# A decoder layer on one core: two rounds of weight rounding moved to other steps, and one pair of maxima matmuls placed ahead of an output projection

## The chip, the core and the metric

The kernel runs on one core of a Trainium2 chip. The metric is the time of one execution on the device, in microseconds; less is better. The engines of the core are TensorE (PE in the rows; PEld is its weight load), VectorE (DVE), ScalarE (ACT), GpSimd (POOL) and SyncE (SP, here the queue that issues most DMAs). Each works through its own list of instructions in order and waits on semaphores.

## What is computed

One post-norm decoder layer on 4 sequences of 512 tokens of width 512: causal self attention with rotary position (16 heads of 32, 8 key and value heads), causal cross attention over the first 512 rows of a context of width 128, and a gated feed-forward of width 1408 whose three weights go through a 4-bit (NF4) quantisation and back. A layer norm follows each of the three.

```python
x = _layernorm(x + _L0_attn_ref(x, wq, wk, wv, wo))            # self attention
x = _layernorm(x + _L0_xattn_ref(x, ctx_512, Wq, Wkv_expand, Wout))
w1, w2, w3 = (nf4_roundtrip(w) for w in (weight1, weight2, weight3))
h = _silu(x @ w1.T) * (x @ w2.T)
x = _layernorm(x + h @ w3.T)
```

## The kernel before

The attention part runs over batches b = 0 to 7 (0 to 3 are the four sequences in self attention, 4 to 7 the same in cross attention; `crossed(b)` is b >= 4) and, in each, over pairs of heads p = 0 to 7. One such step is named (b, p) here. The order of instructions on every engine is written out by hand in these two nested loops; nothing schedules them. The feed-forward follows.

In a step, PE computes the transposed scores of the pair (`scores`, L1027), in four parts 0 to 3 whose exponentials ScalarE takes (`exponential`, L1506); it weighs the values with them (`weigh`, L1054), the last two parts of a pair in the following step; and it computes the scores of the pair two steps ahead (`maxima`, L993, four parts of two matmuls) only so that VectorE can take each row's maximum (L1709 in self, L1703 in cross attention). `turn_maxima` (L1015) transposes these maxima once a step; "from transpose to transpose" below is from one of these to the next. Beside this, a step makes a piece of the next batch (`made`, `make`: q, k and v projections at L979 to L981, transposes at L1066). For self attention POOL rotates the raw q and k (L792, L795, L797) and splits them in high and low parts (L780, L782). In step (b, 1) stands the output projection of the batch before, in two halves (`project_out`), with VectorE's residual add (`add_residual`, L1732 and L1733) and the first moments of the layer norm behind each; the rows are scaled later (`scale_rows`, L1759), in step 5 for b = 5 and 6, and stored by SP (L579).

The weights of the feed-forward are rounded to the 16 levels of NF4 meanwhile, in 48 rounds u. `round_steps` lists the step of each round; step 1 of a batch after the first has two, one in the middle (`mid`) between the halves of the output projection and one at the end (`end`). One round is:

- SP: `load_rows4` (L514) loads the source rows, repeated four times, once PE has read those of the round before; `load_scales` first stores the result of the round before in four DMAs (`store_round`, L527), then loads the scales (L521).
- Four comparison passes over a tile of 128 x 1408 in bf16, at L1484 on ScalarE or L1863 on VectorE (`exceed`). `scalar_passes` says which passes are ScalarE's: pass 0 alone, or 0 and 1 in cross steps 2, 4 and 5, or 0, 1 and 3 in self steps 3 and 4. Pass 3 writes over the source rows, so it comes after the other three.
- PE: `rounding` (L1176), 16 matmuls, 12 for passes 0 to 2 and 4 for pass 3, which wait for the passes.
- VectorE: `scale_rounded` (L1877) adds, scales and so frees the PSUM bank.

The PSUM tile `att_scores_T` has two banks that are given out in turn, in the order that `ring_order` lists; a unit waits until the unit two places ahead of it has been read. PSUM `att_scores` holds the maxima's scores, one bank for each head of the pair. `SELF_ROUNDS` is the number of rounds in self attention; these have their source rows in one buffer (`att_nf_home`), the later ones in another (in `att_probs`).

The loops also load the stacked q and k of the pair three steps ahead (`load_stacks`, L493, L497, L501, six DMAs). For the first pair of a batch this stands behind the rounding's DMAs of its step, otherwise ahead of them.

## Time and profile before

| what | before |
|---|---|
| median of 3 runs | 1099.31 us (1093.14 to 1099.64) |
| the profiled execution | 1097.65 us |
| its span in the profile | 1095.9 us, 17718 instructions |
| PE busy | 1031.4 us (94%) |
| VectorE busy | 760.2 us (69%) |
| ScalarE busy | 486.3 us (44%) |
| GpSimd busy | 432.4 us (39%) |
| mean granted TensorE clock | 0.98 |
| PE waited for VectorE's comparison passes (L1863), inside roundings | 9.0 us in 12 places |
| PE waited for VectorE's scaling (L1877) | 4.7 us in 7 places |
| PE waited for VectorE's residual add (L1733) | 5.0 us in 8 places |
| the 48 roundings' matmuls | from 165 to 785 us |

### The profile page before, as it was taken

The page shows a single profiled execution, that of the slowest core. Times are in us where ns is not written, and L with a number is a line of the kernel's source. Part 1 is how long each engine was busy: PE and PEld are TensorE (multiplying, and loading weights), DVE is VectorE, ACT ScalarE, POOL GpSimd, SP SyncE. Part 2 cuts the span into 40 slices and gives each one's busy share as a digit, 9 for nine tenths or more (in the row PEclk, how much of TensorE's full clock was granted, in tenths as well). Part 3 has the DMA queues.
Part 4 walks back from the last instruction along what each step waited for, and adds up shares of the span by engine and source line. Part 5 has one row for each costly group of instructions (what it writes and reads, how often), then busy time and mean ns, then how long its engine had stood idle before and what let it go on. Part 6 is the DMA issues. An engine that isn't in the chain of part 4 may idle for free.

```text
span 1095.9 us, 17718 instructions
## 1 busy us (share of the span) xinstructions
PE 1031.4 (94%) x6280; PEld 669.7 (61%) x6280; DVE 760.2 (69%) x1684; ACT 486.3 (44%) x587; POOL 432.4 (39%) x462
## 2 busy tenths in 40 slices
PE   8999999998899899999889999999999999999995
PEld 7555554554555454556456656655657888888884
DVE  7788759766856779558866986887776645463635
ACT  4444444654464555555753776585451212111110
POOL 3558666976498455222342324233265100000000
PEclk9899999999999999999999999999999999999998
DMA  6831577386645864647665576648636303010021
GB/s 233 229 102 30 140 190 193 94 235 176 176 123 144 228 175 124 167 105 165 165 149 147 138 185 166 160 127 189 142 69 220 103 1 116 1 45 33 1 77 39
DMA packets 92618, 145.17 MB, mean 132 GB/s; under 512 B 22506, under 2 KB 39794, under 8 KB 92274
## 3 DMA queue, kind: packets, MB, share of 16 engines
q1 hardware_dynamic: 83218, 116.49, 41.0%
q0 software_dynamic: 8000, 26.75, 8.5%
q8 instruction: 51, 0.84, 0.3%
q10 hardware_dynamic: 1312, 0.79, 0.3%
q14 instruction: 37, 0.30, 0.1%
HBM read 78.09 MB, written 23.73 MB: 93 GB/s over the span
## 4 chain that ended last, share of the span: by engine, by line
PE 65%; DVE 15%; DMA 7%; POOL 5%; issue 4%; ACT 3%; SPq 0%; DVEq 0%; ACTq 0%; POOLq 0%
PE att_pv L1054 11%; PE att_pv L1225 7%; PE att_scores L1225 7%; PE att_scores_T L1365 7%; PE att_scores_T L1027 7%; PE att_scores L993 6%; PE att_scores_T L979 5%; PE att_scores_T L981 5%; PE att_scores_T L980 5%; DMA att_nf_home<-nf_reciprocals 3%; DVE att_mx L1709 2%; DVE att_scores L1703 2%; DVE att_nf_zone L1863 2%; DMA att_q_stack<-att_m_rows 1%; PE att_scores_T L1176 1%
## 5 line engine op out<-in xcount | busy, mean ns | idle before, releaser
L1506 ACT ACTIVATE att_probs<-att_scores_T 128x1024 f32<-128x1024 f32 (+2 forms) x256 | 218.3, 883 | 154.5 <-PE att_scores_T L1027 150.7
L1054 PE MATMUL att_pv<-att_probs,att_v 128*32 128x512 f32 (+3 forms) x1024 | 213.7, 533 | 1.4 <-POOL att_probs L851 1.2
L1054 PE MATMUL att_pv<-att_probs,att_ones 128*32 128x512 f32 (+3 forms) x1024 | 213.6, 533 | 0.0
L1709 DVE TENSOR_REDUCE att_mx<-att_scores 128x1 f32<-128x512 f32 x248 | 159.0, 683 | 72.8 <-PE att_scores L993 71.6
L993 PE MATMUL att_scores<-att_k_stack,att_q_stack 96*128 96x256 f32 (+1 forms) x504 | 172.1, 407 | 11.3 <-DVE att_mx L1709 6.8
L1027 PE MATMUL att_scores_T<-att_q_stack,att_k_stack 97*128 97x512 f32 (+2 forms) x512 | 141.5, 387 | 15.1 <-DVE att_nf_zone L1877 4.7
L1703 DVE CUSTOM_DVE_ANT_0 att_scores<-att_scores,att_cmask 128x128 f32<-128x128 f32 (+3 forms) x256 | 120.9, 511 | 42.8 <-PE att_scores L993 41.0
L851 POOL TENSOR_SCALAR_AFFINE_SELECT att_probs<-att_probs 128x256 f32<-128x256 f32 x128 | 57.8, 452 | 219.5 <-ACT att_probs L1506 216.3
L993 PEld LDWEIGHTS att_scores<-att_k_stack,att_q_stack 96*128 96x128 f32 x504 | 91.2, 195 | 55.3 <-DVE att_mx L1709 22.9
L1027 PEld LDWEIGHTS att_scores_T<-att_q_stack,att_k_stack 97*128 97x128 f32 x512 | 87.2, 194 | 55.6 <-DVE att_nf_zone L1877 17.8
L1602 ACT ACTIVATE att_probs<-att_scores 128x512 f32<-128x512 f32 x44 | 26.2, 597 | 203.8 <-PE att_scores L1225 203.8
L1054 PEld LDWEIGHTS att_pv<-att_probs,att_v 128*32 128x32 f32 x1024 | 48.1, 111 | 96.8 <-issue 77.4
L2032 DVE TENSOR_TENSOR att_probs<-att_probs,att_pv 128x512 f32<-128x512 f32 x44 | 30.2, 686 | 106.5 <-PE att_pv L1225 106.5
L1484 ACT ACTIVATE att_nf_zone<-att_probs,att_nf_limits 128x1408 bf16<-128x1408 bf16 x37 | 54.1, 1462 | 39.1 <-DMA att_probs<-nf_x 38.6
L809 POOL TENSOR_TENSOR att_pv_raw<-att_pv_raw,att_sums_turned 128x512 f32<-128x512 f32 x32 | 41.5, 1297 | 67.2 <-DVE att_sums_turned L1726 49.1
L1427 ACT ACTIVATE att_raw<-att_scores_T 128x1024 f32<-128x1024 f32 x35 | 35.5, 1015 | 56.2 <-PE att_scores_T L981 55.0
L979 PE MATMUL att_scores_T<-att_x_hi,att_w_hi 128*128 128x512 f32 x144 | 58.0, 403 | 0.3 <-ACT att_probs L1506 0.2
L979 PE MATMUL att_scores_T<-att_w_hi,att_o_hi 128*128 128x512 f32 x128 | 51.9, 405 | 5.3 <-DVE att_y L1733 2.8
L981 PE MATMUL att_scores_T<-att_x_hi,att_w_lo 128*128 128x512 f32 x144 | 56.5, 392 | 0.0
L980 PE MATMUL att_scores_T<-att_x_lo,att_w_hi 128*128 128x512 f32 x144 | 56.4, 392 | 0.0
L981 PE MATMUL att_scores_T<-att_w_hi,att_o_lo 128*128 128x512 f32 x128 | 50.6, 395 | 0.0
L980 PE MATMUL att_scores_T<-att_w_lo,att_o_hi 128*128 128x512 f32 x128 | 50.5, 394 | 0.0
(262 smaller groups left out, 2096.9 us busy)
## 6 DMA issues: line engine op xcount, KB each, us to landing
att_q_stack<-att_q_hi SPq DMA_DIRECT2D x128, 128.0 KB, 3.3
att_probs<-nf_x SPq DMA_DIRECT2D x28, 352.0 KB, 3.6
att_nf_home<-nf_reciprocals POOLq DMA_DIRECT2D x48, 176.0 KB, 4.8
att_q_stack<-att_q_lo SPq DMA_DIRECT2D x64, 128.0 KB, 3.6
att_k_stack<-att_k_hi SPq DMA_DIRECT2D x64, 128.0 KB, 3.5
att_nf_home<-nf_x SPq DMA_DIRECT2D x20, 352.0 KB, 3.8
w_nf<-att_nf_zone SPq DMA_DIRECT2D x192, 22.0 KB, 2.6
att_k_stack<-att_k_hi SPq DMA_DIRECT2D x64, 64.0 KB, 3.7
```

What stands on the lines that cost most here:

```text
L851: pool.affine_select(out=v, in_=v, compare_op=ALU.is_ge, fill=0.0, base=0, pattern=[[0, 2], [1, P]], channel_multiplier=-1).then_inc(kept, 1)
L979: T.matmul(out, a_hi, b_hi, start=start, stop=False)
L980: T.matmul(out, a_hi, b_lo, start=False, stop=False)
L981: return T.matmul(out, a_lo, b_hi, start=False, stop=stop)
L993: T.matmul(sco[:, r, 0:width], qst[0:96, s, r, P * t:P * t + P], kst[0:96, r if crossed(b) else 0, s, 0:width], start=True, stop=True).the ...
L1027: last = T.matmul(bank[:, at:at + S - q0], kst[0:97, r if crossed(b) else 0, s, P * t:P * t + P], qst[0:97, s, r, q0:S], start=True, stop= ...
L1054: last = T.matmul(pv[HD * j:HD * j + HD, sums, q0:S], lhs, pr[:, at:at + S - q0], start=(t == 0), stop=(t == TT - 1))
L1225: last = T.matmul(bank, ffn_weight(w, f, kt), x[:, kt, :], start=kt == 0 and i == 0, stop=kt == KT - 1 and i == 1)
L1365: last = T.matmul(fpy[:, t, :], h[:, g % 2, P * t:P * t + P], ffn_rows(f), start=f == 0 and i == 0, stop=f == FT - 1 and i == 1)
L1506: A.activation(probs_of(b, r)[:, 1024 * h:1024 * h + w], bank[:, 0:w], ACT.Exp, scale=SCALE).then_inc(st_free, 1)
L1703: V.tensor_tensor_reduce(out=sco[:, r, 0:width], in0=sco[:, r, 0:width], in1=cmask[:, S - width:S], scale=1.0, scalar=NEG, op0=ALU.add, op ...
L1709: V.tensor_reduce(mx[:, p % 2, TT * r + t:TT * r + t + 1], sco[:, r, :], AX.X, ALU.max).then_inc(sc_free, 1)
```

## The change

Three edits, and nothing else is touched.

1. `round_steps` leaves out (5, 5) and (6, 5) and no longer (1, 5) and (2, 5); self attention has 22 rounds in place of 20. The total is 48 as before. Step (4, 5) keeps its round and (3, 5) still has none. Rounds from the fifth on get a number that is one higher at the same step, from (2, 6) on two higher, and (5, 6) and (6, 6) take one back each. In a step of self attention with p = 5 ScalarE has pass 0 and VectorE passes 1, 2 and 3.
2. PE: in steps (4, 1), (5, 1) and (6, 1) the fourth part of the maxima stands between the middle rounding and the second half of the output projection, and not behind that half.
3. VectorE: in the same steps it reduces the fourth part right behind the scaling of that rounding.

```diff
-SELF_ROUNDS = 20
+SELF_ROUNDS = 22
...
         for p in range(NP):
-            if b < B and p == 5 or b == B - 1 and p > 4 or (b, p) in ((1, 0), (B, 0)):
+            if b == B - 1 and p > 4 or (b, p) in ((1, 0), (B, 0), (B + 1, 5), (B + 2, 5)):
                 continue
             steps += [(b, p)] * (2 if p == 1 and b > 1 else 1)
...
                         if mid is not None:
                             rounding(mid)
+                        between = crossed(b) and mid is not None
+                        if between:
+                            maxima(*fore, 3)
                         project_out(b - 1, 1)
-                        maxima(*fore, 3)
+                        if not between:
+                            maxima(*fore, 3)
...
                         if mid is not None:
                             scale_rounded(mid)
+                        between = crossed(b) and mid is not None
+                        if between:
+                            maxima(*fore, 3)
                         moments(b - 1, 0)
                         for what in made(b + 1, p):
                             cut_raw(b + 1, what)
                         exceeds(end, (1, 2, 3))
                         add_residual(b - 1, 1)
-                        maxima(*fore, 3)
+                        if not between:
+                            maxima(*fore, 3)
```

VectorE's list around step (1, 5), before. The first row is the scaling of step (1, 4)'s round and the second the last shuffle of that step; the reductions behind it are the maxima of (1, 4)'s fourth part, of the whole of (1, 5) and of the first part of (1, 6).

```order
L1877 SCALAR_TENSOR_TENSOR att_nf_zone<-att_scores_T,att_nf_home 128x352
L1656 STREAM_SHUFFLE att_swapped<-att_raw 128x1024
L1709 TENSOR_REDUCE att_mx<-att_scores 128x1 x12
L1715 STREAM_TRANSPOSE att_sums_turned<-att_pv_raw 128x512
L1719 RECIPROCAL att_rcp<-att_sums_turned 64x16 x2
```

The same place in the changed kernel, whose line numbers are 4 higher here:

```order
L1881 SCALAR_TENSOR_TENSOR att_nf_zone<-att_scores_T,att_nf_home 128x352
L1660 STREAM_SHUFFLE att_swapped<-att_raw 128x1024
L1713 TENSOR_REDUCE att_mx<-att_scores 128x1 x4
L1867 TENSOR_SCALAR att_nf_zone<-att_nf_home,att_nf_limits 128x1408 x2
L1713 TENSOR_REDUCE att_mx<-att_scores 128x1 x2
L1867 TENSOR_SCALAR att_nf_home<-att_nf_home,att_nf_limits 128x1408
L1881 SCALAR_TENSOR_TENSOR att_nf_zone<-att_scores_T,att_nf_home 128x352
L1713 TENSOR_REDUCE att_mx<-att_scores 128x1 x6
```

Passes 1 and 2 stand behind the second part of the maxima of (1, 5), pass 3 behind the third, and the scaling ahead of the fourth. Step (2, 5) is alike.

SP's list in step (5, 5), before. Ahead of it stand the DMAs of step (5, 4); the first three rows are those of (5, 5)'s round (with the store of (5, 4)'s result), then come the stacks of pair (6, 0), the store of the normed rows, and the stacks of pair (6, 1), which belong to step (5, 6). The DMAs of (5, 6)'s round stand right behind the piece.

```order
L514 DMA att_probs<-nf_x 128x1x1408
L527 DMA w_nf<-att_nf_zone 32x352 x4
L521 DMA att_probs<-nf_dequantised_rows 128x352
L493 DMA att_q_stack<-att_q_hi 32x2x512 x2
L497 DMA att_k_stack<-att_k_hi 32x2x512 x2
L493 DMA att_q_stack<-att_q_lo 32x2x512
L497 DMA att_k_stack<-att_k_lo 32x2x512
L579 DMA x_after_cross<-att_y 128x4x512
L493 DMA att_q_stack<-att_q_hi 32x2x512 x2
L497 DMA att_k_stack<-att_k_hi 32x2x512 x2
L493 DMA att_q_stack<-att_q_lo 32x2x512
L497 DMA att_k_stack<-att_k_lo 32x2x512
```

In the changed kernel:

```order
L493 DMA att_q_stack<-att_q_hi 32x2x512 x2
L497 DMA att_k_stack<-att_k_hi 32x2x512 x2
L493 DMA att_q_stack<-att_q_lo 32x2x512
L497 DMA att_k_stack<-att_k_lo 32x2x512
L579 DMA x_after_cross<-att_y 128x4x512
L493 DMA att_q_stack<-att_q_hi 32x2x512 x2
L497 DMA att_k_stack<-att_k_hi 32x2x512 x2
L493 DMA att_q_stack<-att_q_lo 32x2x512
L497 DMA att_k_stack<-att_k_lo 32x2x512
L514 DMA att_probs<-nf_x 128x1x1408
L527 DMA w_nf<-att_nf_zone 32x352 x4
L521 DMA att_probs<-nf_dequantised_rows 128x352
```

The round's DMAs are gone from (5, 5); (5, 4)'s result is stored in (5, 6). On PE, the place of the second edit in step (5, 1), before (the first half of the projection ends above the roundings' rows, the second half begins below them; its last three rows and what follows stand at the end of the piece):

```order
L1176 MATMUL att_scores_T<-att_nf_zone,att_nf_steps 32x352 x12
L1176 MATMUL att_scores_T<-att_probs,att_nf_steps 32x352 x4
L979 MATMUL att_scores_T<-att_w_hi,att_o_hi 128x512
...
L979 MATMUL att_scores_T<-att_w_hi,att_o_hi 128x512
L980 MATMUL att_scores_T<-att_w_lo,att_o_hi 128x512
L981 MATMUL att_scores_T<-att_w_hi,att_o_lo 128x512
L993 MATMUL att_scores<-att_k_stack,att_q_stack 128x512 x2
L1054 MATMUL att_pv<-att_probs,att_v 32x512 x2
```

and in the changed kernel:

```order
L1176 MATMUL att_scores_T<-att_nf_zone,att_nf_steps 32x352 x12
L1176 MATMUL att_scores_T<-att_probs,att_nf_steps 32x352 x4
L993 MATMUL att_scores<-att_k_stack,att_q_stack 128x512 x2
L979 MATMUL att_scores_T<-att_w_hi,att_o_hi 128x512
L980 MATMUL att_scores_T<-att_w_lo,att_o_hi 128x512
```

The pair of matmuls at L993 has moved up past the 24 matmuls of the projection's second half.

## Rows read from the trace of the kernel before

**Rows 1.** PE timeline, step (5,5): start us, length us, row; [idle before <-releaser]
```profile
641.19 0.33 PE L1176 MATMUL att_scores_T<-att_probs,att_nf_steps 128*32 128x352 bf16 x4 [1.04 <-DVE att_probs L1863]
642.45 0.67 PE L1027 MATMUL att_scores_T<-att_q_stack,att_k_stack 97*128 97x512 f32 x2 [0.32 <-DVE att_nf_zone L1877]
```

**Rows 2.** Windows view, transpose to transpose, from step (5,4) and from step (5,5)
```profile
core 0: us, PE busy (x) PEld busy (x) DVE busy (x) ACT busy (x) POOL busy (x), PEclk, DMA share, GB/s
625.38:634.22 8.84, 8.57 (x76) 4.92 (x73) 8.13 (x24) 8.44 (x11) 2.55 (x5) 1.00 0.34 93
634.22:644.50 10.28, 8.93 (x76) 4.95 (x73) 9.32 (x26) 8.07 (x10) 5.90 (x8) 0.95 0.68 174
```

**Rows 3.** DVE from the timeline, step (5,5)
```profile
638.57 0.72 DVE L1863 TENSOR_SCALAR att_nf_zone<-att_probs,att_nf_limits 128x1408 bf16<-128x1408 bf16 x1
640.97 0.99 DVE L1759 TENSOR_SCALAR att_y<-att_y,att_mean_var,att_newton 128x512 f32<-128x512 f32 x2
```

**Rows 4.** SP queue, DVE and PE from the timeline, steps (5,5) to (5,7)
```profile
641.99 0.39 SPq L579 DMA_DIRECT2D x_after_cross<-att_y  x1
648.16 0.58 SPq L514 DMA_DIRECT2D att_probs<-nf_x  x1
...
651.87 1.08 DVE L1863 TENSOR_SCALAR att_nf_zone<-att_probs,att_nf_limits 128x1408 bf16<-128x1408 bf16 x2 [3.10 <-DMA att_probs<-nf_x]
...
654.13 0.58 DVE L1863 TENSOR_SCALAR att_probs<-att_probs,att_nf_limits 128x1408 bf16<-128x1408 bf16 x1
...
662.63 0.33 PE L1176 MATMUL att_scores_T<-att_probs,att_nf_steps 128*32 128x352 bf16 x4 [0.75 <-DVE att_probs L1863]
```

**Rows 5.** PE from the timeline, step (5,1)
```profile
593.31 0.50 PE L979 MATMUL att_scores_T<-att_w_hi,att_o_hi 128*128 128x512 f32 x1 [0.74 <-DVE att_y L1733]
...
599.01 0.62 PE L993 MATMUL att_scores<-att_k_stack,att_q_stack 96*128 96x512 f32 x2
```

**Rows 6.** Windows view, transpose to transpose, from steps (1,5), (2,5) and (1,7)
```profile
217.01:225.37 8.36, 8.32 (x53) 3.65 (x49) 5.15 (x8) 4.14 (x5) 7.93 (x5) 1.00 0.65 168
332.03:340.33 8.30, 8.29 (x54) 3.66 (x50) 5.15 (x8) 4.14 (x5) 7.95 (x5) 1.00 0.58 128
241.55:250.62 9.07, 9.07 (x70) 4.16 (x67) 6.98 (x12) 6.44 (x7) 5.84 (x8) 1.00 0.86 258
```

**Rows 7.** POOL from the timeline, around step (1,5)
```profile
217.30 2.38 POOL L782 TENSOR_TENSOR att_k_lo<-att_turned,att_k_hi 128x1024 fp32r<-128x1024 f32 x1
219.82 2.37 POOL L792 TENSOR_TENSOR att_turned<-att_raw,att_rope_tab 128x1024 f32<-128x1024 f32 x1
222.34 2.39 POOL L795 TENSOR_TENSOR att_swapped<-att_swapped,att_rope_tab 128x1024 f32<-128x1024 f32 x1
```

**Rows 8.** DVE timeline, steps (1,4) and (3,1): comparison passes beside a POOL instruction
```profile
205.48 2.77 DVE L1863 TENSOR_SCALAR att_nf_zone<-att_nf_home,att_nf_limits 128x1408 bf16<-128x1408 bf16 x1
...
379.81 2.30 DVE L1863 TENSOR_SCALAR att_nf_zone<-att_nf_home,att_nf_limits 128x1408 bf16<-128x1408 bf16 x2
```

**Rows 9.** POOL from the timeline, at the same places
```profile
205.46 2.40 POOL L792 TENSOR_TENSOR att_turned<-att_raw,att_rope_tab 128x1024 f32<-128x1024 f32 x1
...
380.28 1.44 POOL L815 TENSOR_TENSOR att_o_lo<-att_pv_raw,att_o_hi 128x512 fp32r<-128x512 f32 x1
```

**Rows 10.** DVE and PE from the timeline, step (1,5)
```profile
217.53 2.68 DVE L1709 TENSOR_REDUCE att_mx<-att_scores 128x1 f32<-128x512 f32 x4 [1.12 <-PE att_scores L993]
...
221.15 0.73 PE L993 MATMUL att_scores<-att_k_stack,att_q_stack 96*128 96x512 f32 x2
```

**Rows 11.** Windows view: the same PE work ending steps (1,1) and (2,1)
```profile
167.29:173.39 6.10, 5.26 (x23) 1.82 (x24) 5.75 (x22) 2.05 (x2) 3.69 (x5) 0.72 0.84 229
282.00:286.50 4.50, 3.67 (x22) 1.35 (x23) 4.32 (x13) 2.05 (x2) 3.88 (x4) 1.00 0.56 160
```

**Rows 12.** ACT and PE from the timeline, step (1,6)
```profile
232.64 1.47 ACT L1484 ACTIVATE att_nf_zone<-att_nf_home,att_nf_limits 128x1408 bf16<-128x1408 bf16 x1 [4.89 <-DMA att_nf_home<-nf_x]
...
238.53 0.73 PE L1027 MATMUL att_scores_T<-att_q_stack,att_k_stack 97*128 97x512 f32 x2 [1.14 <-DVE att_nf_zone L1877]
```

## The prediction

> **What bounds the kernel now.** I read the busy shares first. PE is busy in 1031.4 of the 1095.9 us of the profiled span (the profile's table), so nearly every microsecond that a step gains or loses is one of PE's own work or of a hole in it. Then I read who PE waits for, and went to the places of the change in the timeline of each engine. I name a step (b, p): batch b (0 to 3 self, 4 to 7 cross attention) and head pair p, both from zero, so the "sixth steps" are p = 5.
>
> In step (5,5) PE stands still 1.04 us inside the rounding, for VectorE's last comparison pass, and 0.32 us behind it, for the bank that VectorE's scaling frees [rows 1]. Transpose to transpose, that stretch takes 10.28 us where step (5,4), with the same kind of work on PE (two halves of a projection of keys, one rounding), takes 8.84, and its mean granted clock is 0.95 against 1.00 [rows 2]. Step (6,5) has the same two waits. In steps (4,1), (5,1) and (6,1) PE stands still 0.74 us between the rounding and the second half of the output projection, because VectorE's residual add has not freed the bank [rows 5]. These are the holes that the two edits aim at.
>
> **The change, part by part.**
>
> *Rounding out of (5,5) and (6,5).* PE loses 16 matmuls. A rounding in a bare step costs PE 0.7 us: 9.07 us in (1,7) with one, 8.36 in (1,5) without [rows 6]. With the waits (10.28 - 8.84 = 1.44) that makes 2.1 us a step, if nothing else comes late. But something does. In (5,5) the SP queue waits for the layer norm's scaled rows, stores them at 641.99, issues the six stack loads of the next pair, and only then, at 648.16, the source rows of step (5,6)'s rounding; they land at 651.87, where VectorE has waited 3.10 us for them [rows 4]. Behind them stand two passes (1.08), the fourth maxima (about 1.2) and the third pass, which ends at 654.7; a PE that came earlier would wait for it. One step on, PE waits 0.75 us for VectorE's third pass in (5,7), at 662.63 [rows 4]. So from (5,6) on the SP chain sets the pace, and PE keeps only what this chain gains. The chain starts at VectorE's last scaled row. Ahead of that row the change removes two passes, 0.72 us [rows 3] and 0.58 us (the length of the uncontended one in [rows 4]), less the overlap of their ends: 1.2 us. I take 1.2 us a step, 2.4 in all; bounds 0.7 (the matmuls alone) and 3.7 (2.1 and 1.6 for the clock, priced below).
>
> *Rounding into (1,5) and (2,5).* PE gains the same 16 matmuls, 0.7 us each. ScalarE takes one pass, VectorE three (in (5,5) it was two each), and SP six DMAs. In its queue they stand ahead of the stack loads of the next batch's first pair, which wait for POOL's keys anyway and are wanted a step later, so I charge nothing for them. What decides is POOL. It is busy 7.93 and 7.95 us of the 8.36 and 8.30 of these two stretches, and only 5.84 of the 9.07 in (1,7) [rows 6]. A comparison pass beside a POOL instruction does not run: the one that starts at 205.48 takes 2.77 us and ends at 208.25, 0.39 us after POOL's 205.46 + 2.40 = 207.86; the pair at 379.81 ends at 382.11, 0.39 after POOL's 380.28 + 1.44 = 381.72 [rows 8, 9]. The pair shows too that POOL's next instruction gets in between two passes that stand back to back. The Trainium skill has this as a rule (SBUF — State Buffer, section "SBUF: two separate sides"): a VectorE instruction in a two-port mode and a GpSimd instruction hold one pair of ports in turn, each for its whole length, and the loser is blocked; its figure of about 0.115 us from release to start would put a 0.58 us pass 0.7 us behind POOL's end in place of 0.39. By that figure, an estimate, each of the two steps would be 0.3 us dearer than by my rows.
>
> Now step (1,5) by the clock of before. VectorE's second maxima are through at 217.53 + 2.68 / 2 = 218.9 [rows 10]. Pass 1 waits for POOL's 217.30 + 2.38 = 219.68 [rows 7] and ends at 220.1. Pass 2 stands behind POOL's next, which ends at 219.82 + 2.37 = 222.2 and slips 0.1: it ends at 222.7. The third maxima (half of 2.68) end at 224.0. Pass 3 stands behind POOL's 222.34 + 2.39 = 224.7, slipped 0.1: it ends at 225.2. PE finishes its weighing at about 221.1, waits for pass 2 until 222.7, runs 12 matmuls, waits again until 225.2, and runs the last 4 until 225.5. Only then come the fourth maxima, which stood at 221.15 [rows 10]. That is 4.3 us, of which 0.7 are matmuls. Step (2,5) has the same POOL instructions, equally close, so 4.3 again: 8.6.
>
> Two corrections. In (1,6) ScalarE waits 4.89 us for source rows that land at 232.64, and PE then waits 1.14 us for the bank of the rounding [rows 12]. That landing hangs on SP's queue and not on PE, so a PE that comes 4 us later no longer meets this wait: -1.1. And two waits of 1.6 and 2.5 us within 4.3 us are more than what preceded the low clock elsewhere: at the end of (1,1), with PE idle for 6.10 - 5.26 = 0.84 us, the granted clock was 0.72 in the mean (1.2 GHz for a part of the stretch), and the work took 6.10 us; in (2,1), with 0.83 us idle, it was 1.00 and the same work took 4.50 [rows 11]. I charge 1.6 us in each of the two steps: +3.2. Bounds for the two steps together: 1.4 (two clean roundings as in (1,7)) and 11.8 (8.6 and 3.2, nothing given back).
>
> *The fourth maxima between round and projection, (4,1), (5,1), (6,1).* PE's two matmuls, 0.62 us, move from 599.01 into the hole of 0.74 us ahead of 593.31 [rows 5]. Their input has long landed, and the banks they write were freed by VectorE's third maxima microseconds before. VectorE takes their two reductions 6 us earlier, ahead of the moments; what is queued behind (moments, the low part of x, the passes for the end rounding) delays nobody, since that rounding comes only after the projection's whole second half and the weighing. About 0.55 us each: -1.7. Bounds 0 and 2.2 (the whole 0.74 three times).
>
> Sum: 8.6 - 1.1 + 3.2 - 2.4 - 1.7 = +6.6 us. Against its own execution of 1097.65 us (span and what lies around it) that gives 1104.3. The three runs shown have a median of 1099.31, 1.7 us above that execution, and lie between 1093.14 and 1099.64, so a run can differ by as much as the sum.
>
> **Rivals.**
> (A) The passes in (1,5) and (2,5) slip through, as in (1,7): self pays 1.4 us, and cross gains its full 2.1 twice, so 1.4 - 4.2 - 1.7 = -4.5: 1093.2, and down to 1090 with the clock of (5,5) and (6,5) given back. For it: passes run in 0.58 us where POOL is free. Against: POOL is free for only 0.4 us in these stretches. It decides at the second pass: if that one does not wait for a whole POOL instruction, step (1,5) loses 2.5 us less. This is the rival on the faster side. 2 in 10.
> (B) The waits come, but the clock does not fall: 6.6 - 3.2 = +3.4, 1101.0. For it: (2,1), with the same idle time as (1,1), kept its clock [rows 11]. 2 in 10.
> (C) The waits and the low clock come in self, but cross is not held by the SP queue, since stores ahead of the stack loads are gone: gain 2 x 3.7 = 7.4 in place of 2.4, so +1.6, 1099.2. 1 in 10.
> (D) PE's delay in self makes further things late (the next batch's stacks or layer norm), a second pair of waits like the first: 6.6 + 5 or more, above 1110. 0.8 in 10.
> My forecast keeps 4.2 in 10.
>
> **How the numbers follow.** The time is the forecast's, 1104.3. The range takes in B and C and most of A and ends short of D: 1092 to 1109. A measurement of this kernel can tell about 1% from no change, 11 us: faster needs under 1088.3, which only the lower end of A with a fast execution reaches (0.03); slower needs over 1110.3, which is D (0.08); the rest is 0.89.
>
> **What would show it.** In the changed trace, comparison passes of 1 to 3 us in (1,5) and (2,5), each ending 0.4 us after a POOL instruction; two waits of PE inside each of these roundings, 1.6 and 2.1 to 2.5 us, for VectorE; granted clock under 1.00 behind them; 12.7 us or more in place of 8.36 and 8.30. In (5,5) and (6,5) a stretch of about 8 us, but a new wait of PE of some 2 us in the roundings of (5,6) and (6,6), with the source rows landing only 1.2 us earlier against PE's own work. In (x,1) no wait ahead of the projection's second half. Passes of 0.6 us in (1,5) would make the forecast wrong, and so would a rounding in (5,6) that does not wait.

## Result: 0.7% slower, and the profile of the changed kernel

| what | before | after |
|---|---|---|
| median of 19 runs each | 1096.16 us (1091.56 to 1102.68) | 1106.23 us (1097.26 to 1109.52) |
| ratio, after to before | | 1.0071, 95% interval 1.0054 to 1.0088 |
| the profiled execution, its span | 1097.65, 1095.9 us | 1104.53, 1102.8 us |
| PE busy | 1031.4 us | 1037.2 us |

The ratio times the median of before is 7.8 us more, with an interval of 5.9 to 9.6; the two profiled spans differ by 6.9. The sum of the prediction was 6.6. PE is busy for 5.8 us longer with the same work, and idle in sum for only 1.1 us longer (65.6 us in place of 64.5). That is a net figure: the two moved roundings bring 7.1 us of new waits, shown below, and nearly as much idle time goes elsewhere, so that what is left in the sum is mostly low clock.

In step (1,5), which was 8.36 us [rows 6], PE now has a rounding with two waits in it. PE, DVE and POOL from the timeline of the changed kernel (start, length, row):

```profile
221.31 0.63 PE L1176 MATMUL att_scores_T<-att_nf_zone,att_nf_steps 128*32 128x352 bf16 x12 [1.63 <-DVE att_nf_zone L1867]
223.90 0.49 PE L1176 MATMUL att_scores_T<-att_nf_home,att_nf_steps 128*32 128x352 bf16 x4 [1.96 <-DVE att_nf_home L1867]
...
217.19 3.98 DVE L1867 TENSOR_SCALAR att_nf_zone<-att_nf_home,att_nf_limits 128x1408 bf16<-128x1408 bf16 x2
221.09 1.27 DVE L1713 TENSOR_REDUCE att_mx<-att_scores 128x1 f32<-128x512 f32 x2
222.28 1.47 DVE L1867 TENSOR_SCALAR att_nf_home<-att_nf_home,att_nf_limits 128x1408 bf16<-128x1408 bf16 x1
...
215.79 2.38 POOL L782 TENSOR_TENSOR att_k_lo<-att_turned,att_k_hi 128x1024 fp32r<-128x1024 f32 x1
218.31 2.47 POOL L792 TENSOR_TENSOR att_turned<-att_raw,att_rope_tab 128x1024 f32<-128x1024 f32 x1
220.92 2.45 POOL L795 TENSOR_TENSOR att_swapped<-att_swapped,att_rope_tab 128x1024 f32<-128x1024 f32 x1
```

Read it from POOL. L792 ends at 218.31 + 2.47 = 220.78, the second pass at 217.19 + 3.98 = 221.17, 0.39 later. L795 ends at 223.37, the third pass at 222.28 + 1.47 = 223.75, 0.38 later. Each of PE's matmul groups starts 0.15 us behind a pass. Step (2,5) has waits of 1.56 and 1.96 us. The windows view, transpose to transpose, of (1,5), (2,5), (5,5), (5,6), (6,5) and (6,6):

```profile
core 0: us, PE busy (x) PEld busy (x) DVE busy (x) ACT busy (x) POOL busy (x), PEclk, DMA share, GB/s
215.44:230.48 15.04, 11.45 (x69) 5.27 (x66) 10.87 (x12) 5.50 (x6) 14.31 (x11) 0.77 0.81 214
334.08:349.50 15.42, 11.90 (x70) 5.33 (x66) 10.80 (x12) 5.50 (x6) 14.68 (x11) 0.78 0.66 161
...
643.81:651.27 7.46, 7.46 (x59) 4.43 (x56) 6.97 (x19) 4.98 (x8) 5.12 (x7) 1.00 0.50 96
651.27:665.74 14.47, 12.91 (x93) 8.30 (x90) 9.39 (x30) 7.74 (x10) 2.17 (x5) 1.00 0.96 238
734.15:741.61 7.46, 7.46 (x63) 4.43 (x59) 6.97 (x22) 4.99 (x8) 5.07 (x7) 1.00 0.55 107
741.61:757.77 16.16, 14.21 (x101) 9.07 (x97) 9.93 (x30) 8.40 (x11) 2.86 (x6) 0.91 0.83 222
```

The self steps are 6.7 and 7.1 us longer. In each PE is busy for 11.45 or 11.90 us where (1,7), with a rounding too, took 9.07 [rows 6]: at a mean granted clock of 0.77 and 0.78 (1.2 GHz from the middle of the rounding on, for not quite half of the step) the same matmuls take 2.4 and 2.8 us more. (5,5) fell from 10.28 [rows 2] to 7.46 us, and (5,6) rose from 13.01 to 14.47. What holds PE there, from the timeline of the changed kernel (SP queue, DVE, PE):

```profile
650.43 0.39 SPq L579 DMA_DIRECT2D x_after_cross<-att_y  x1
...
656.02 0.58 SPq L514 DMA_DIRECT2D att_probs<-nf_x  x1
...
660.17 1.08 DVE L1867 TENSOR_SCALAR att_nf_zone<-att_probs,att_nf_limits 128x1408 bf16<-128x1408 bf16 x2 [4.59 <-DMA att_probs<-nf_x]
...
661.73 0.63 PE L1176 MATMUL att_scores_T<-att_nf_zone,att_nf_steps 128*32 128x352 bf16 x12 [0.44 <-ACT att_nf_zone L1488]
663.15 0.33 PE L1176 MATMUL att_scores_T<-att_probs,att_nf_steps 128*32 128x352 bf16 x4 [0.78 <-DVE att_probs L1867]
```

The chain of [rows 4] is there again, with a wait for the source rows of 4.59 us in place of 3.10. In (6,6) the same two waits (0.84 and 0.79 us) are followed by a low clock, so the step is 3.3 us longer than before.

Transposes on PE mark the steps in both traces. Summed over what the edits touch, after less before:

| steps | measured us | forecast us |
|---|---|---|
| (1,5), (2,5) | +6.7, +7.1 | +4.3 each, +3.2 for the clock of both |
| (1,6) | -1.4 | -1.1 |
| (1,7) | +1.0 | 0 |
| (5,5) to (5,7) | -1.45 | -1.2 |
| (6,5) to (6,7) | -0.8 | -1.2 |
| (4,1), (6,1) | -0.51, -0.46 | -0.55 each |
| (5,1) | -1.27 (before had a low clock there) | -0.55 |

Counting (5,1) as the other two this is +9.7 where +6.6 was forecast. Of the remaining -2.8 us of the spans' difference, 0.8 is the low clock that the kernel before had in (5,1). The other 2.0 lie in steps that no edit touches, (1,1) with -4.2 and (3,2) with +4.1 the largest. The first of these is scatter: (1,1) stands ahead of the first edit of every kernel in this document, and in the 13 profiled executions it took between 20.55 and 26.49 us. Two near its ends, from the first and the second kernel of the section on the SP queue; the longer has a lower clock and 3 us of idle time of PE:

```profile
150.16:176.63 26.47, 23.49 (x117) 13.46 (x114) 16.92 (x37) 6.67 (x7) 17.66 (x20) 0.89 0.70 188
152.19:172.74 20.55, 20.20 (x118) 12.96 (x114) 12.23 (x30) 6.67 (x7) 11.95 (x13) 1.00 0.74 193
```

### The profile page after: what moved, and what is told of

The parts are those of the page before. It is cut to its first block, busy times and chain, and to the rows that moved or that the text cites. A ratio compares the mean times of both kernels' runs of the same rounds, so it can differ in the third digit from the quotient of the medians.

```text
span 1102.8 us, 17718 instructions
## 1 busy us (share of the span) xinstructions
PE 1037.2 (94%) x6280; PEld 672.9 (61%) x6280; DVE 761.2 (69%) x1686; ACT 484.3 (44%) x585; POOL 434.0 (39%) x462
## 4 chain that ended last, share of the span: by engine, by line
PE 69%; DVE 15%; DMA 6%; issue 4%; POOL 2%; ACT 2%; SPq 1%; DVEq 0%; ACTq 0%; POOLq 0%
PE att_pv L1054 12%; PE att_scores_T L1027 7%; PE att_pv L1225 7%; PE att_scores L1225 7%; PE att_scores_T L1369 7%; PE att_scores L993 7%; PE att_scores_T L979 5%; PE att_scores_T L980 5%; PE att_scores_T L981 5%; DVE att_scores L1707 2%; DVE att_mx L1713 2%; DVE att_nf_zone L1867 2%; DMA att_q_stack<-att_m_rows 2%; DMA att_nf_home<-nf_reciprocals 2%; PE att_scores_T L1176 2%
## 5 line engine op out<-in xcount | busy, mean ns | idle before, releaser
L993 PE MATMUL att_scores<-att_k_stack,att_q_stack 96*128 96x256 f32 (+1 forms) x504 | 173.7, 411 | 12.1 <-DVE att_mx L1713 7.7
L1027 PE MATMUL att_scores_T<-att_q_stack,att_k_stack 97*128 97x512 f32 (+2 forms) x512 | 143.8, 392 | 13.2 <-DMA att_q_stack<-att_m_rows 5.7
L993 PEld LDWEIGHTS att_scores<-att_k_stack,att_q_stack 96*128 96x128 f32 x504 | 91.7, 196 | 56.2 <-DVE att_mx L1713 22.0
L1488 ACT ACTIVATE att_nf_zone<-att_probs,att_nf_limits 128x1408 bf16<-128x1408 bf16 x33 | 48.3, 1462 | 39.2 <-DMA att_probs<-nf_x 38.9
```

The costliest lines, as they stand in the source:

```text
L993: T.matmul(sco[:, r, 0:width], qst[0:96, s, r, P * t:P * t + P], kst[0:96, r if crossed(b) else 0, s, 0:width], start=True, stop=True).the ...
L1027: last = T.matmul(bank[:, at:at + S - q0], kst[0:97, r if crossed(b) else 0, s, P * t:P * t + P], qst[0:97, s, r, q0:S], start=True, stop= ...
```

## Experiments

Each was timed in 5 rounds beside the kernel before; ratios are to that, with a 95% interval.

### The two edits apart

`k1_rounds` has only the moved roundings (`between = False` in both places), `k2_maxima` only the moved maxima (`SELF_ROUNDS` and `round_steps` of before).

> The two roundings moved, the fourth maxima left where they were. My theory, by the sum of the prediction: 8.6 - 1.1 + 3.2 - 2.4 = 8.3 us over the kernel before (ratio 1.0075), with the two PE waits of 1.6 and 2.0 us in (1,5) and in (2,5), and the wait of 0.74 us for the residual's bank again in (4,1), (5,1) and (6,1). Rival (the two edits interact, or the maxima bring nothing in the end): the time of the changed kernel, 6.9 us over before in the profiled executions (ratio about 1.006 to 1.007), and no difference from it that can be measured.

> The kernel before with the fourth maxima of the second cross steps between rounding and output projection, and nothing else. My theory: the 0.74 us wait goes in (4,1), (5,1) and (6,1), each of these steps is 0.5 us shorter, and the whole is 1.5 us faster (ratio 0.9986). Rival: the wait only moves to the next thing that VectorE brings late (the moments and the low part of x are now behind two more reductions), ratio 1.000 or above.

Measured: the roundings alone 1104.3 us, ratio 1.0085 (1.0064 to 1.0105), 9.3 us; 8.3 were expected. The maxima alone 1096.06 us, ratio 1.000 (0.9981 to 1.002). Its interval holds the -1.4 us and zero. In the profile of the second (4,1) takes 20.08 us in place of 20.56 and (6,1) 20.05 in place of 20.53, and in that of the first both stay at 20.53 and 20.50. So the move gives 0.5 us where it stands, three times, and the wait doesn't come back elsewhere; in the time this is too small to be shown. The loss is the roundings'.

### Is it POOL that holds the passes?

```diff
+                n = 32 if unit[1] in (2, 3) and unit[2] == "q1" else S
...
-                pool.tensor_tensor(rsw, rsw, sin, ALU.mult).then_inc(sine, 1)
+                pool.tensor_tensor(rsw[:, :, 0:n], rsw[:, :, 0:n], sin[:, :, 0:n], ALU.mult).then_inc(sine, 1)
```

(and the same for the other two of `rotate`, and for one division in each step)

> The changed kernel with POOL's work in (1,5) and (2,5) cut: the three rotation instructions on the second queries (L792, L795, L797) of batches 2 and 3 take 64 of 1024 columns, and the division of the first piece in each of the two steps (L765) 64 of 704, so this part of the computation is left out; every instruction, wait and DMA stays. My theory (VectorE's comparison passes are blocked by POOL instructions): passes of 0.6 us, no PE wait of over 0.3 us in either rounding, both steps 9.1 us in place of 15.04 and 15.42, granted clock 1.00 in them, 10 to 12 us less in all (ratio to before about 0.996). Rival 1 (the source rows or VectorE's own work ahead of the passes are late): both waits stay, ratio 1.006. Rival 2 (the low clock has another cause than the waits): the waits go, 3.6 us a step, but the two low stretches of 6.8 us stay, and the steps take about 11.5 us, ratio 1.000.

Measured: 1101.53 us, ratio 1.0049 (1.0024 to 1.0073), a miss where about 0.996 was expected. The step (1,5) did nearly what was expected, (2,5) did not. Windows view of the two, then rows of DVE, PE, POOL and the SP queue in them (a line number is 1 or 2 higher here):

```profile
core 0: us, PE busy (x) PEld busy (x) DVE busy (x) ACT busy (x) POOL busy (x), PEclk, DMA share, GB/s
217.85:227.77 9.92, 9.13 (x70) 4.19 (x67) 7.79 (x12) 5.50 (x6) 9.11 (x12) 1.00 0.71 191
333.74:347.78 14.04, 10.82 (x69) 4.30 (x65) 8.08 (x12) 5.50 (x6) 7.12 (x11) 0.88 0.85 199
```

```profile
222.60 0.57 DVE L1869 TENSOR_SCALAR att_nf_home<-att_nf_home,att_nf_limits 128x1408 bf16<-128x1408 bf16 x1
...
223.32 0.33 PE L1178 MATMUL att_scores_T<-att_nf_home,att_nf_steps 128*32 128x352 bf16 x4 [0.79 <-DVE att_nf_home L1869]
...
337.79 1.57 DVE L1869 TENSOR_SCALAR att_nf_home<-att_nf_home,att_nf_limits 128x1408 bf16<-128x1408 bf16 x1
...
337.92 1.05 POOL L781 CAST att_q_hi<-att_turned 128x1024 fp32r<-128x1024 f32 x1
...
339.51 0.33 PE L1178 MATMUL att_scores_T<-att_nf_home,att_nf_steps 128*32 128x352 bf16 x4 [1.07 <-DVE att_nf_home L1869]
343.58 0.73 PE L995 MATMUL att_scores<-att_k_stack,att_q_stack 96*128 96x512 f32 x2 [2.15 <-DMA att_k_stack<-att_k_lo]
...
336.88 0.60 SPq L501 DMA_DIRECT2D att_k_stack<-att_k_lo  x1
...
336.35 0.54 POOL L759 DMA_DIRECT2D att_nf_home<-w_t  x1
336.88 1.05 POOL L761 DMA_DIRECT2D att_nf_home<-nf_reciprocals  x2
```

With POOL's instructions small, the third pass of (1,5) takes 0.57 us, the wait of 1.63 us ahead of the first matmuls is gone, and the clock stays at 1.00: 9.92 us in place of 15.04. This shows that POOL held them. But 0.79 us of the second wait stay, although nothing blocks: on VectorE a maxima reduction of 1.27 us stands between the passes, and PE's 12 matmuls are done before the third pass has begun. In (2,5) the third pass is blocked once more, by a cast of the next unit that now comes earlier: the cast ends at 337.92 + 1.05 = 338.97, the pass at 339.36, 0.39 later, as in [rows 8, 9]. And PE then waits 2.15 us for a stack load of (3,0). In SP's queue that load is 3.13 us behind the step's transposes (336.88, the step begins at 333.75) and was 1.89 in the kernel before, so the rounding's DMAs cost it 1.2 us. That alone would not be felt. Transfers to the low part of the k stacks take 6.3 us from issue to landing in this stretch and 2.4 in the kernel before (medians of the DMA views); with 2.4 it would have landed at 339.3, ahead of PE. In the same stretch POOL issues the three transfers of the next piece, earlier than it would with its full work; in the changed kernel they come later, the median is 2.3 us, and PE has no such wait. So this wait comes with the shortened POOL work and is no cost of the change. That the three transfers are what slowed the load is my reading of the times; it was not tested by itself.

### Three passes on ScalarE

```diff
-    return (0, 1, 3) if b < B - 1 and p in (3, 4) else (0,)
+    return (0, 1, 3) if b < B - 1 and p in (3, 4, 5) else (0,)
```

> The changed kernel with three of the four passes of (1,5) and (2,5) on ScalarE, which idles 6.46 us there, and one on VectorE. My theory: VectorE's single pass ends 0.4 us behind POOL's low part (218.17), ScalarE's second pass ends at 221.4 and its third at 222.9, so PE starts at 221.4 (wait 1.7 us as now) and its second wait falls from 1.96 to about 0.9 us: 1 us a step if the clock falls as now, 2 to 3 us a step if two waits of 2.6 us in sum keep the clock; 2 to 6 us less in all than the changed kernel (ratio to before 1.001 to 1.005). Rival (ScalarE's exponentials come late behind its passes): the steps are as long as now or longer, ratio 1.006 or above.

Measured: 1100.68 us, ratio 1.0041 (1.0014 to 1.0068), inside the expected 1.001 to 1.005. The waits came as expected, 1.75 and 0.82 us, and they came alike in both steps. The steps did not:

```profile
219.56 0.63 PE L1176 MATMUL att_scores_T<-att_nf_zone,att_nf_steps 128*32 128x352 bf16 x12 [1.75 <-issue]
221.01 0.33 PE L1176 MATMUL att_scores_T<-att_nf_home,att_nf_steps 128*32 128x352 bf16 x4 [0.82 <-ACT att_nf_home L1488]
...
338.06 0.63 PE L1176 MATMUL att_scores_T<-att_nf_zone,att_nf_steps 128*32 128x352 bf16 x12 [1.75 <-issue]
339.51 0.33 PE L1176 MATMUL att_scores_T<-att_nf_home,att_nf_steps 128*32 128x352 bf16 x4 [0.82 <-ACT att_nf_home L1488]
```

```profile
core 0: us, PE busy (x) PEld busy (x) DVE busy (x) ACT busy (x) POOL busy (x), PEclk, DMA share, GB/s
213.57:228.39 14.82, 12.25 (x69) 5.10 (x65) 6.79 (x10) 8.32 (x8) 14.09 (x11) 0.77 0.84 226
332.06:343.95 11.89, 9.32 (x69) 4.07 (x65) 6.70 (x10) 8.32 (x8) 11.24 (x10) 1.00 0.67 163
```

This pair is the cleanest price of the clock in the study: 69 PE instructions in each, idle for 2.57 us in each, and 12.25 us busy at a granted clock of 0.77 against 9.32 at 1.00, so 2.9 us. It also shows that the waits inside a step don't decide alone whether the clock falls. The two later kernels with this form of the passes have the same waits within 0.02 us in both steps, and took 13.15 and 14.77 us in one, 14.51 and 13.13 in the other, at 0.87, 0.77, 0.76 and 0.87: of six such steps one kept its clock.

### Does a slower form of the pass slip past POOL?

```diff
-                V.tensor_scalar((over + [x4])[k], x4, limits[:, k:k + 1], 2.0, ALU.is_gt, ALU.mult).then_inc(over_vec, 1)
+                if ROUND_STEPS[u] in ((1, 5), (2, 5)):
+                    V.scalar_tensor_tensor((over + [x4])[k], x4, limits[:, k:k + 1], x4, ALU.is_gt, ALU.mult).then_inc(over_vec, 1)
+                else:
+                    V.tensor_scalar((over + [x4])[k], x4, limits[:, k:k + 1], 2.0, ALU.is_gt, ALU.mult).then_inc(over_vec, 1)
```

> The changed kernel with VectorE's three passes of (1,5) and (2,5) as a scalar_tensor_tensor, which multiplies the comparison by the source rows in place of 2.0 (so these two roundings compute something else). It has two tensor inputs, and I expect about 1.5 us for it (1408 columns; an estimate from 0.52 us for 352) in place of 0.58 us where nothing blocks. My theory (the fast form shares ports with POOL and is held until POOL's instruction ends): this slower form isn't held, each of the three takes 1.5 us whatever POOL does, the first two end at 220.1 in place of 221.17 by the clock of the changed kernel, the third at 222.9 in place of 223.75, and PE's waits fall from 3.59 to 2.7 us a step, 1 us a step faster although each instruction does the same work at under half the speed. Rival (POOL and VectorE contend for bandwidth, or the passes start late for another reason): the passes take over 2 us each beside POOL and end later than now, PE's waits grow by 1 us or more a step.

Measured: 1111.55 us, ratio 1.0139 (1.0097 to 1.0181), and (1,5) and (2,5) at 18.29 and 19.04 us. My theory for this form fell: PE's waits in (1,5) grew from 3.59 to 6.30 us (3.69 and 2.61), as the rival said. DVE and POOL in (1,5):

```profile
219.59 6.04 DVE L1868 SCALAR_TENSOR_TENSOR att_nf_zone<-att_nf_home,att_nf_limits 128x1408 bf16<-128x1408 bf16 x2
221.87 3.76 DVE L1868 SCALAR_TENSOR_TENSOR att_nf_zone<-att_nf_home,att_nf_limits 128x1408 bf16<-128x1408 bf16 x1
...
218.09 2.38 POOL L782 TENSOR_TENSOR att_k_lo<-att_turned,att_k_hi 128x1024 fp32r<-128x1024 f32 x1
220.60 3.55 POOL L792 TENSOR_TENSOR att_turned<-att_raw,att_rope_tab 128x1024 f32<-128x1024 f32 x1
224.29 3.54 POOL L795 TENSOR_TENSOR att_swapped<-att_swapped,att_rope_tab 128x1024 f32<-128x1024 f32 x1
```

The first pass can't run until L782 ends at 220.47, and then is through by about 221.9. L792, issued at 220.60, is held for that time: it takes 3.55 us in place of 2.47 and ends at 224.15. The second pass ends at 221.87 + 3.76 = 225.63, 1.48 us behind that, and L795 in turn takes 3.54. Those 1.48 us are about the whole length that I estimated for such a pass (1.5), so it made no progress beside L792, which speaks against the rival's reason, a sharing of bandwidth. So the two engines take turns, whole instruction by whole instruction, and both are held; with the fast form POOL's share of it was 0.1 us. The Trainium skill (SBUF — State Buffer, section "SBUF: two separate sides") lists a VectorE instruction with two SBUF inputs beside the two-port forms as a taker of that lock; this run agrees, with 3.55 us for an instruction of 2.4, and I had read only half of that rule. Whether a slow form with one input would pass was not tried.

### The SP queue

```diff
-                        if u is not None:
+                        if u is not None and (b, p) not in AHEAD:
...
+                    if (b, p + 1) in AHEAD:
+                        u = rounds_of(b, p + 1)[1]
+                        load_rows4(u)
+                        load_scales(u)
                     if b > 0 and p == stored_at(b):
                         store(b - 1)
```

`AHEAD` is (4,5), (5,6) and (6,6).

> The changed kernel with SP's queue written in another order at three places: the source rows and scalers of the roundings of (4,5), (5,6) and (6,6) are asked for ahead of the store of the layer norm's rows (and so ahead of the next pair's stack loads), one step earlier than now. My theory (this chain holds PE in (5,6) and (6,6)): the rows of (5,6) are asked for at about 646 in place of 656.02 and have landed when VectorE comes to them, its waits of 4.59 and 4.99 us go, PE's two waits in each of these roundings (0.44 and 0.78 in (5,6)) go, 1.2 to 1.6 us a step, and where the clock fell in (6,6) 1.6 more: 3 to 4.5 us less than the changed kernel (ratio to before 1.003 to 1.004). Rival (VectorE's passes are held by its own queue, the wait for the rows only covers it): the rows land early, PE's waits stay within 0.3 us of what they are, ratio as the changed kernel's, 1.006 to 1.007.

Measured: 1103.74 us, ratio 1.0055 (1.0028 to 1.0082), so not told from the changed kernel by the time. By steps: (5,6) 12.92 us (14.47 in the changed kernel), (5,7) 7.52 (8.40), (6,6) 12.89 (16.16), the PE waits for passes gone from (5,6) and (6,6) and down to 0.25 us in (5,7); but (4,5) went from 9.32 to 11.83. The theory holds for the two places of the change, and the third place was a mistake. PE and the SP queue there, in this kernel:

```profile
563.41 0.79 PE L998 MATMUL att_scores<-att_k_stack,att_q_stack 96*128 96x256 f32 x2 [2.27 <-DMA att_k_stack<-att_k_lo]
...
559.51 0.61 SPq L498 DMA_DIRECT2D att_k_stack<-att_k_lo  x1
```

The rows and scalers now stand ahead of the store and the stack loads, and here the stacks are what PE wants next: it waits 2.27 us for the last of them.

> The kernel before (roundings as it has them) with the moved fourth maxima and the SP order of the run above. My theory: 1.5 us from the maxima, and from the SP order the 0.75 us wait of PE in (5,7) and the like in (6,7), 1.5 to 2.5 us: 3 to 4 us faster than before (ratio 0.9965 to 0.997). Rival (PE is held in (5,5) and (6,5), where nothing of the SP order changes, and what the maxima bring is lost to scatter): ratio 0.999 to 1.001.

Measured: 1101.18 us, ratio 1.0031 (1.000 to 1.0061): a miss. (4,5) was 12.50 us, with a wait of PE of 2.93 us for the stacks. And with the rounding still in (5,5), PE ran on to (5,7) and waited there 3.13 us for a pass whose source rows were asked for at 656.76, behind twelve stack loads: the late link had moved one step on.

> The changed kernel with both corrections: ScalarE takes three of the four passes in (1,5) and (2,5), and the SP order of the first run of this call. By the profile of the first correction alone 4 us less than the changed kernel, and 3 more by the second: ratio to before 1.000 to 1.001. Rival (each correction works only where the other's hole was): ratio 1.004, as with the first alone.

Measured: 1100.22 us, ratio 1.0024 (0.9996 to 1.0052), between the two expectations, with (4,5) at 10.82 us.

> The changed kernel with three of the four passes of (1,5) and (2,5) on ScalarE and the SP order at (5,6) and (6,6) alone. My theory: by the run with SP's order at three places (ratio 1.0024) less the 2.5 us that the third place, (4,5), cost in it: ratio 1.000. Rival ((4,5) was a low clock by chance and not the order): no difference, 1.0024 again.

Measured: 1098.38 us, ratio 1.0003 (0.9982 to 1.0024), (4,5) back at 9.33 us. The interval reaches the rival's 1.0024, so it is the step and not the time that answers it: (4,5) took 9.27 to 10.29 us in the ten profiled kernels without the order there, and 10.82 to 12.50 in the three with it. The change with both its holes narrowed is level with the kernel before.

### The cross half alone, and the version that beats both

```diff
-            if b < B and p == 5 or b == B - 1 and p > 4 or (b, p) in ((1, 0), (B, 0)):
+            if b < B and p == 5 or b == B - 1 and p > 4 or (b, p) in ((1, 0), (B, 0), (B + 1, 5), (B + 2, 5)):
```

with `SELF_ROUNDS = 20`, so that the two roundings go behind the last one, and `AHEAD = ((B + 1, 6), (B + 2, 6))` in the first of the two.

> The cross half of the change with its SP chain mended, and nothing in self: roundings leave (5,5) and (6,5) but go behind the last one, into (7,1) (which then has two) and (7,2); the fourth maxima as in the change; source rows and scalers of (5,6) and (6,6) asked for ahead of the store, (4,5) left as it was (there the same order cost 2.5 us). My theory, from the steps of the run of the changed kernel with the three places mended: (5,5) to (5,7) 27.9 us in place of 31.8, (6,5) to (6,7) 27.9 in place of 31.9, maxima 1.4 less, two plain roundings late in the program 2.1 more: 7.2 us faster than before, ratio 0.9935. Rival (the late roundings collide with the load of the next weights or the clock falls behind them): they cost 5 us or more, ratio 0.997 or above.

> The same without the SP order, so the cross half of the change alone. My forecast's term (the SP chain lets through only 1.2 us a step): -2.4 - 1.4 + 2.1 = 1.7 us faster than before, ratio 0.9985, with PE waits in the roundings of (5,6) and (6,6). Rival C of the prediction (cross gains 3.7 a step): 7.4 + 1.4 - 2.1 = 6.7 us faster, ratio 0.994, and no difference to the kernel with the SP order.

Measured: without the SP order 1096.51 us, ratio 0.9997 (0.9973 to 1.0021); with it **1090.31 us, ratio 0.9932 (0.9906 to 0.9957)**. In the first, PE has its waits in (5,6). Timeline of that kernel, SP queue, DVE and PE:

```profile
646.35 0.57 SPq L514 DMA_DIRECT2D att_probs<-nf_x  x1
...
650.54 1.08 DVE L1867 TENSOR_SCALAR att_nf_zone<-att_probs,att_nf_limits 128x1408 bf16<-128x1408 bf16 x2 [5.26 <-DMA att_probs<-nf_x]
...
652.11 0.63 PE L1176 MATMUL att_scores_T<-att_nf_zone,att_nf_steps 128*32 128x352 bf16 x12 [1.08 <-ACT att_nf_zone L1488]
653.52 0.33 PE L1176 MATMUL att_scores_T<-att_probs,att_nf_steps 128*32 128x352 bf16 x4 [0.78 <-DVE att_probs L1867]
```

With the rows asked for ahead of the store neither DVE nor PE waits (line numbers are 5 higher here), and the step is 12.88 us:

```profile
643.14 1.08 DVE L1872 TENSOR_SCALAR att_nf_zone<-att_probs,att_nf_limits 128x1408 bf16<-128x1408 bf16 x2
...
648.66 0.63 PE L1181 MATMUL att_scores_T<-att_nf_zone,att_nf_steps 128*32 128x352 bf16 x12
649.10 0.33 PE L1181 MATMUL att_scores_T<-att_probs,att_nf_steps 128*32 128x352 bf16 x4
...
638.81:651.69 12.88, 12.56 (x93) 8.38 (x90) 9.57 (x30) 7.72 (x10) 2.15 (x5) 1.00 0.99 228
```

(5,5) to (5,7) are 29.3 us together and (6,5) to (6,7) 28.1, against 31.8 and 31.9 before. (7,1) and (7,2) are 1.2 and 2.2 us longer for the late roundings; 2.1 in all were expected. With 1.5 for the maxima, the steps that the edits touch gain 4.3 us in this profiled execution, where 7.2 were expected and the ratio says 7.5 (4.7 to 10.3). So the time came out as expected although the terms did not, and that is luck in part: the profiled execution was 1.3 us slower than the median of its kernel, and part of the rest lies in steps that no edit touches. The effect of the SP order itself is clear of this: the two intervals, with it and without it, do not overlap. So these two steps of cross attention are worth freeing, but only if the SP chain goes too, and if the roundings find a place that costs less than (1,5) did. POOL was busy for 3.24 of the 20.04 us of (7,1) and 1.56 of the 9.38 of (7,2).

## Why the prediction was right, and where its terms were off

The forecast, 1104.3 us within 1092 to 1109, holds the 1106.2, and the outcome that it gave 0.89, within 1% of the kernel before, is what came. As a change it was 6.6 us, measured 7.8, with an interval that is clear of zero.

- **Passes blocked in (1,5) and (2,5), 4.3 us a step.** Right in mechanism and size: waits of 1.63 + 1.96 and 1.56 + 1.96 us, and 0.7 us of matmuls, make 4.3 and 4.2. The run with small POOL instructions shows the cause of all but 0.8 us a step; those are VectorE's own order, which the prediction had put down to POOL. Passes ended 0.38 and 0.39 us behind POOL's instructions, as in the rows of before; the 0.7 us that the prediction estimated from the Trainium skill's 0.115 us (SBUF — State Buffer, section "SBUF: two separate sides") came in none of them. Rival A needed the second pass to run past a POOL instruction, and it never did.
- **The clock, 1.6 us a step.** It fell in both, and in both again in two other profiled kernels with these passes (0.77, 0.77 and 0.77, 0.78), so rival B is out, but the term was too small: 2.4 and 2.8 us by PE's busy time, 2.9 in the pair of the ScalarE run. I had taken it from a shorter fall: 0.72 over 6.10 us [rows 11] is 3.4 us at half speed, 0.77 over 15.04 is 6.9. Why this one is longer was not tested. That is 2.0 us of the 3.1 by which the touched steps exceed the sum.
- **The wait in (1,6) absorbed, -1.1.** -1.4. But a step on, in (1,7), PE met a new wait of 0.96 us for the row of maxima (`att_m_rows`), which I had not seen coming. (1,7) took 9.10 to 10.40 us in the eight profiled kernels with a rounding in (1,5), 9.09 to 9.35 in the five without.
- **SP's six DMAs charged at nothing.** They delay the stack loads of (3,0) by 1.2 us in the small-POOL run and by 1.9 in the changed kernel (3.81 us behind the step's transposes in place of 1.89), and no wait of PE was traced to that delay alone.
- **Cross held by the SP chain, -1.2 a step.** -1.45 and -0.8. As the forecast said, the source rows land 1.3 us earlier against PE's own work (16.4 us behind the transposes of (5,5) in place of 17.7), and PE waits in the roundings of (5,6) and (6,6), 1.2 and 1.6 us where it had said some 2. The order of the chain is shown to be the cause: moved, the same steps gain 2.5 and 3.7 us. Rival C expected that without moving anything, and the cross half alone refutes it with 0.9997. The clock fell in (6,6), which I had not allowed for there.
- **Maxima, -0.55 three times.** About 0.5 by the steps; not to be shown in the time.

The sum of the spans, 6.9, is nearer to 6.6 than its terms deserve, and that is luck: the touched steps cost 9.7, and 2.8 came back in places that the sum says nothing of, of which the -4.2 of (1,1) is scatter, since no edit stands ahead of it.

Step (3,1) is the open end, and it is rival D's: that PE's delay in self makes further things late. No edit stands in it. It took 23.33 us in the cross half alone and 29.88 in the ScalarE run:

```profile
379.62:402.95 23.33, 22.06 (x142) 14.04 (x138) 17.42 (x25) 11.04 (x12) 15.07 (x15) 1.00 0.57 160
379.00:408.88 29.88, 25.26 (x141) 14.55 (x138) 20.77 (x25) 11.04 (x12) 20.57 (x21) 0.89 0.72 182
```

In the longer one PE waited 1.77 us for a comparison pass, and its granted clock was 0.89 against 1.00. Over all 13 profiled executions, the five kernels without a rounding in (1,5) and (2,5) took 23.3 to 24.2 us there; of the eight with it three took as little (the changed kernel 23.40), and five took 26.6 to 29.9, each with such a wait of 0.6 to 2.1 us. So D did not come in the profiled execution of the changed kernel, but it may come in others; (1,1) varies nearly as much with no edit ahead of it, and no run tests (3,1) by itself. The prediction's price for D, 6.6 + 5, gives about 1109 and not "above 1110".

## What to carry to other kernels

Before work is moved to a step where an engine is idle, look at which other engine works there without a pause: VectorE idled in (1,5), but POOL did not, and each pass cost a whole POOL instruction. A hole on the bottleneck engine is closed only when the chain behind it is moved too: here the freed step gave its gain back to a DMA that stood behind a store and six other DMAs in its queue, and only when it was put ahead did the two freed steps show in the time, as 0.7%. A stall also covers other lateness (0.8 us of the second wait in (1,5) was VectorE's own order), so cost the next late thing before you count on a removal.

## What the runs showed of the hardware

- Two steps with the same PE instructions and the same waits (1.75 and 0.82 us) ran at a granted clock of 0.77 and 1.00, 14.82 and 11.89 us. In this step the two waits are a risk of 2.9 us for the clock, not a fixed price.
- A VectorE instruction with two SBUF inputs and a GpSimd instruction hold up each other: 3.55 us for a GpSimd instruction of 2.4, and 1.48 us behind its end for the VectorE one. With the fast one-input form only VectorE loses noticeably (0.39 us behind POOL's end, POOL 0.1 longer).
- The load of the source rows (352 KB) took 4.2 us from issue to landing at 656.02 in the changed kernel, and 5.9 at 656.76 in the kernel before with the moved maxima and the SP order, behind twelve stack loads.
